# Adapter kernel on one core: who issues the loads of W_up, who writes the first seed, when the sort's tail runs, and the order of work in the first tiles

## The reference

```python
Wd = W_down[stream]; bd = b_down[stream]; Wu = W_up[stream]
bu = b_up[stream]; g = ln_w[stream]; b = ln_b[stream]
h = jnp.einsum('bsh,bhk->bsk', hidden_states, Wd) + bd[:, None, :]
h = jax.nn.gelu(h, approximate=False)
h = jnp.einsum('bsk,bkh->bsh', h, Wu) + bu[:, None, :]
h = residual + h                     # residual = hidden_states
mean = jnp.mean(h, axis=-1, keepdims=True)
var = jnp.mean(jnp.square(h - mean), axis=-1, keepdims=True)
h = (h - mean) * jax.lax.rsqrt(var + LN_EPS)
return h * g[:, None, :] + b[:, None, :]
```

## Time and profile before

| | before |
|---|---|
| median of 3 runs | 139.09 us (139.05 to 139.56) |
| profiled execution, its own time | 139.21 us |
| its span, first to last instruction | 137.2 us |
| mean granted PE clock | 0.987 of full speed |
| PE busy | 126.6 us (92%) |
| DVE busy | 112.9 us (82%) |
| POOL busy | 104.5 us (76%) |
| ACT busy | 85.1 us (62%) |

### The profile page before, as it was taken

One profiled execution on the slowest core, in us unless ns is written; L12 is line 12 of the kernel. 1 busy time (PEld: TensorE's weight loads), 2 busy tenths in 40 slices (PEclk: granted clock), 3 DMA queues, 4 the chain that ended last, 5 costly groups with the idle time before them and its releaser, 6 DMA issues.

```text
span 137.2 us, 4086 instructions
## 1 busy us (share of the span) xinstructions
PE 126.6 (92%) x850; PEld 112.5 (82%) x851; DVE 112.9 (82%) x273; ACT 85.1 (62%) x177; POOL 104.5 (76%) x117
## 2 busy tenths in 40 slices
PE   6788799999899999999999999999999999999830
PEld 6687667799799999999999999999999999998610
DVE  1899588788898888888988897889788978897992
ACT  0768576536966666666676666666666666666600
POOL 7047933438599888888888888888888898889960
PEclk9999999999999999999999999999999999999995
DMA  1967999995554354554555545455556533331365
GB/s 45 336 203 244 272 259 280 286 232 159 151 166 133 99 151 153 155 155 153 153 155 153 153 155 153 153 153 153 153 153 158 148 76 76 81 76 38 87 163 176
DMA packets 13200, 21.94 MB, mean 160 GB/s; under 512 B 2297, under 2 KB 3842, under 8 KB 13186
## 3 DMA queue, kind: packets, MB, share of 16 engines
q1 hardware_dynamic: 8802, 15.74, 41.6%
q10 hardware_dynamic: 4384, 6.05, 14.5%
HBM read 13.39 MB, written 8.65 MB: 161 GB/s over the span
## 4 chain that ended last, share of the span: by engine, by line
PE 70%; DVE 11%; POOL 6%; ACT 5%; issue 3%; DMA 2%; POOLq 1%; ACTq 1%; DVEq 0%
PE hg_ps L891 28%; PE y_ps L923 28%; PE xT_ps L877 8%; PE hg_ps L900 5%; POOL res L396 2%; DMA itok_all_i<-in_itok_B_dram 2%; DVE r_stats L704 1%; ACT xT_hi L463 1%; DVE hb L692 1%; ACT y_ps L480 1%; DVE res L740 1%; DVE scaled L725 1%; POOL slot_same L367 1%; POOL slot_step L366 1%; POOLq L210 1%
## 5 line engine op out<-in xcount | busy, mean ns | idle before, releaser
L396 POOL TENSOR_TENSOR res<-normed,lnb_rows 128x512 f32<-128x512 f32 x31 | 39.8, 1285 | 11.9 <-ACT normed L488 11.9
L379 POOL TENSOR_TENSOR xb<-x_sb,bu_rows 128x512 f32<-128x512 f32 x33 | 42.7, 1296 | 2.9 <-DMA x_sb<-in_x_dram 2.3
L468 ACT ACTIVATE g<-hb 128x256 f32<-128x256 f32 x33 | 13.8, 418 | 35.7 <-DVE hb L692 35.7
L704 DVE BATCH_NORM_STATS2 r_stats<-y_ps 128x6 f32<-128x512 f32 x33 | 23.0, 696 | 6.8 <-issue 6.1
L923 PE MATMUL y_ps<-wu_hi,gT_hi 128*128 x66 | 23.3, 434 | 1.4 <-ACT gT_hi L473 1.2
L684 DVE TENSOR_TENSOR xT_lo<-xT_ps,xT_hi 128x512 fp32r<-128x512 f32 x33 | 22.8, 690 | 2.1 <-ACT xT_hi L463 2.1
L385 POOL TENSOR_TENSOR rstd<-var_eps,half_neg 128x1 f32<-128x1 f32 x33 | 18.2, 551 | 7.9 <-DVE var_eps L713 7.8
L891 PE MATMUL hg_ps<-wd_hi,xT_hi 128*128 x132 | 24.1, 304 | 0.0
L725 DVE SCALAR_TENSOR_TENSOR scaled<-y_ps,r_mv,lnw_rows 128x512 f32<-128x512 f32 x31 | 22.9, 743 | 0.0
L488 ACT ACTIVATE normed<-scaled,rstd 128x512 f32<-128x512 f32 x31 | 22.3, 722 | 0.0
L891 PE MATMUL hg_ps<-wd_lo,xT_hi 128*128 x132 | 21.0, 282 | 0.0
(11 more groups left out here) (88 smaller groups left out, 148.0 us busy)
## 6 DMA issues: line engine op xcount, KB each, us to landing
x_sb<-in_x_dram SPq DMA_DIRECT2D x64, 128.0 KB, 2.8
out_dram<-res ACTq DMA_DIRECT2D x33, 128.0 KB, 2.4
out_dram<-res SPq DMA_DIRECT2D x33, 128.0 KB, 2.5
wd<-in_L_cond_W_down_dram ACTq DMA_DIRECT2D x3, 512.0 KB, 4.9
wu<-in_L_cond_W_up_dram SPq DMA_DIRECT2D x3, 512.0 KB, 6.3
lnw_rows<-in_L_cond_ln_w_dram SPq DMA_DIRECT2D x1, 768.0 KB, 7.9
lnb_rows<-in_L_cond_ln_b_dram SPq DMA_DIRECT2D x1, 768.0 KB, 9.3
x_sb<-in_x_dram ACTq DMA_DIRECT2D x2, 128.0 KB, 2.8
```

The lines of the kernel that those rows point to most:

```text
L379: pool.tensor_tensor(xb[:, c % DEEP, :], x_sb[:, c % FAR, :], bu_rows[:, ds(e * H, H)], ALU.add).then_inc(xb_ready, 1)
L396: pool.tensor_tensor(res[:, c % FAR, :], normed[:, c % DEEP, :], lnb_rows[:, ds(e * H, H)], ALU.add).then_inc(res_ready, 1)
L704: dve.bn_stats(r_stats[:, c % DEEP, :], y_ps[c % YBANKS][:]).then_inc(stats_ready, 1)
```

## The change

1. **Loads of W_up.** ACT issues all three, behind its two halves of x and behind wd_high(2) in program order. For their experts it reads seven table entries, `io_table[5:12]`, with one register load ahead of wd_high(2); DVE now writes the experts to free third entries of `io_table` instead of `wu_from`. SP reads twelve entries with one register load and issues x for tiles 2 to 5 in a row.
2. **First seed.** DVE writes seed(0), behind down_bias(0); it has a semaphore of its own, `seeded_first`. w_up_low(0) and g_lo(0) follow, then down_bias(1).
3. **Sort's tail.** POOL does add_bias for tiles 0, 1 and 2 first, then the six instructions of the tail.
4. **Order in the head.** ACT: wu_high(1) is ahead of gelu(1), x_hi(3) ahead of gelu(2); g_hi(5), gelu(6), x_hi(8) and seed(6) stand ahead of rescale(2) and rescale(3). DVE: stats(0) comes after g_lo(1) and x_lo(3); mean_var(1) and variance(1) come after x_lo(4). PE: up(1) and up(2) take the products in the usual order; two warm-up matmuls ahead of down(0) are gone.

The core of the diff:

```diff
@@ -295,22 +295,16 @@
 
 
             head_regs = [sp.alloc_register(f"head{i}") for i in range(4)]
-            from_regs = [sp.alloc_register(f"from{i}") for i in range(E)]
+            next_regs = [sp.alloc_register(f"next{i}") for i in range(12)]
 
             sp.wait_ge(slots_ready, 1)
             sp.reg_load(head_regs, io_table[0:1, 0:4])
             for t in range(2):
                 load_half(sp, t, 0, sp.snap(head_regs[3 * t], min_val=0, max_val=B - 1))
             sp.wait_ge(slots_ready, 2)
-            sp.reg_load(from_regs, wu_from[0:1, 0:E])
-            from_expert = [sp.snap(reg, min_val=0, max_val=E - 1 - slot) + slot for slot, reg in enumerate(from_regs)]
-            load_w_up(sp, 0, from_expert[0])
-            load(2, 2, entries(2, 0, 2))
-            load_w_up(sp, 1, from_expert[1])
-            load(3, 3, entries(3, 0, 2))
-            load_w_up(sp, 2, from_expert[2])
-            for t in range(4, 6):
-                load(t, t, entries(t, 0, 2))
+            sp.reg_load(next_regs, io_table[0:1, 5:17])
+            for t in range(2, 6):
+                load(t, t, [sp.snap(reg, min_val=0, max_val=B - 1) for reg in next_regs[3 * t - 5:3 * t - 3]])
             sp.dma_start(lnw_rows[:], rows_of(ln_w, P)).then_inc(lnw_in, 16)
             load(6, 6, entries(6, 0, 2))
             sp.dma_start(lnb_rows[:], rows_of(ln_b, P)).then_inc(lnb_in, 16)
...
+            pool.wait_ge(slots_ready, 2)
+            pool.wait_ge(bu_last_ready, 1)
+            pool.wait_ge(bu_ready, E - 1)
+            for t in range(3):
+                add_bias(t, t)
+
...
-            for t in range(3):
-                add_bias(t, t)
             add_bias(3, 3)
...
@@ -518,24 +515,28 @@
             wd_high(1)
             for t in range(2):
                 load_half(act, t, 1, act.snap(head_regs[3 * t], min_val=0, max_val=B - 1))
+            from_regs = [act.alloc_register(f"from{i}") for i in range(3 * E - 2)]
+            act.wait_ge(slots_ready, 2)
+            act.reg_load(from_regs, io_table[0:1, 5:3 * E + 3])
             wd_high(2)
+            for slot in range(E):
+                load_w_up(act, slot, act.snap(from_regs[3 * slot], min_val=0, max_val=E - 1 - slot) + slot)
             for e in range(E - 1):
                 keep_up_bias(e)
             x_hi(0, 0)
             x_hi(1, 1)
             for part in range(len(bd_banks)):
                 keep_down_bias(part)
-            seed(0, 0)
             wu_high(0)
             gelu(0, 0)
             g_hi(0, 0)
             x_hi(2, 2)
+            wu_high(1)
             gelu(1, 1)
-            wu_high(1)
             seed(1, 1)
             g_hi(1, 1)
+            x_hi(3, 3)
             gelu(2, 2)
-            x_hi(3, 3)
             wu_high(2)
             g_hi(2, 2)
             seed(2, 2)
@@ -556,24 +557,26 @@
             x_hi(7, 7)
             seed(5, 5)
             rescale(1, 1)
+
+            g_hi(5, 5)
+            gelu(6, 6)
+            x_hi(8, 8)
+            seed(6, 6)
             rescale(2, 2)
+            rescale(3, 3)
 
             def body(t, c):
 
                 seed(t, c)
-
-                if from_tile(t, 2):
-                    g_hi(t - 1, c - 1)
-                if from_tile(t, STORE_B_LAG):
-                    store(t - STORE_B_LAG, c - STORE_B_LAG)
+                g_hi(t - 1, c - 1)
+                store(t - STORE_B_LAG, c - STORE_B_LAG)
                 gelu(t, c)
                 x_hi(t + 2, c + 2)
-                if from_tile(t, 3):
-                    rescale(t - 3, c - 3)
+                rescale(t - 3, c - 3)
 
             act.wait_ge(slots_ready, 3)
-            for t in range(STORE_B_LAG, STORE_B_LAG + 2):
-                body(t, t)
+            store(0, 0)
+            body(STORE_B_LAG + 1, STORE_B_LAG + 1)
             tiles(act, body, STORE_B_LAG + 2, TILES - 3)
...
             dve.memset(io_table[0:1, 2:3], 0)
+            dve.memset(io_table[0:1, 14:15], 0)
...
@@ -649,7 +653,7 @@
             link(dve.tensor_scalar(tile_expert[:], key_filled[:, 1:1 + SLOTS:2], B.bit_length() - 1, RANGE // B - 1,
                                    ALU.logical_shift_right, ALU.bitwise_and))
 
-            dve.tensor_tensor(wu_from[:], first_expert, top_row[:], ALU.min)
+            dve.tensor_tensor(io_view[:, 1:1 + E, 2], first_expert, top_row[:], ALU.min)
...
@@ -745,28 +749,29 @@
             x_lo(1, 1)
             dve.wait_ge(bd_ready, len(bd_banks))
             down_bias(0, 0)
-            down_bias(1, 1)
+            dve.wait_ge(xb_ready, 1)
+            dve.tensor_copy(y_ps[0][:], xb[:, 0, :]).then_inc(seeded_first, 1)
             w_up_low(dve, 0).then_inc(wu_lo_ready, 1)
             g_lo(0, 0)
+            down_bias(1, 1)
             x_lo(2, 2)
-
-            stats(0, 0)
-            dve.wait_ge(stats_ready, 1)
             w_up_low(dve, 1).then_inc(wu_lo_ready, 1)
             down_bias(2, 2)
             g_lo(1, 1)
+            x_lo(3, 3)
+
+            stats(0, 0)
+            dve.wait_ge(stats_ready, 1)
+            w_up_low(dve, 2).then_inc(wu_lo_ready, 1)
             mean_var(0, 0)
+            g_lo(2, 2)
             variance(0, 0)
-            x_lo(3, 3)
-
+            down_bias(3, 3)
             stats(1, 1)
             dve.wait_ge(stats_ready, 2)
-            w_up_low(dve, 2).then_inc(wu_lo_ready, 1)
-            g_lo(2, 2)
+            x_lo(4, 4)
             mean_var(1, 1)
-            down_bias(3, 3)
             variance(1, 1)
-            x_lo(4, 4)
             scale(0, 0)
...
@@ -903,20 +910,16 @@
             def up(t, c, e):
 
                 w0 = e * (KB * H)
-                early = isinstance(t, int) and 0 < t < E
                 pe.wait_ge(ghi_ready, t + 1)
                 if isinstance(t, int) and t < E:
                     pe.wait_ge(wu_hi_ready, t + 1)
-                pe.wait_ge(seeded, t + 1)
-                parts = [(gT_hi, wu_hi), (gT_lo, wu_hi), (gT_hi, wu_lo)] if early else [
-                    (gT_hi, wu_hi), (gT_hi, wu_lo), (gT_lo, wu_hi)]
-                for n, (g_half, w_half) in enumerate(parts):
-                    if w_half is wu_lo and isinstance(t, int) and t == 0:
-                        pe.wait_ge(wu_lo_ready, 1)
-                    if w_half is wu_lo and isinstance(t, int) and t == 1:
-                        pe.wait_ge(wu_lo_ready, 2)
-                    if w_half is wu_lo and isinstance(t, int) and t == 2:
-                        pe.wait_ge(wu_lo_ready, 3)
+                if isinstance(t, int) and t == 0:
+                    pe.wait_ge(seeded_first, 1)
+                else:
+                    pe.wait_ge(seeded, t)
+                for n, (g_half, w_half) in enumerate(((gT_hi, wu_hi), (gT_hi, wu_lo), (gT_lo, wu_hi))):
+                    if w_half is wu_lo and isinstance(t, int) and t < E:
+                        pe.wait_ge(wu_lo_ready, t + 1)
                     if g_half is gT_lo:
                         pe.wait_ge(glo_ready, t + 1)
...
@@ -928,10 +931,10 @@
             pe.wait_ge(slots_ready, 2)
             transpose_x(0, 0)
             transpose_x(1, 1)
-            warm_up(WARM_UPS[3], hg_ps[0])
             pe.wait_ge(wd_hi_ready, E)
             down(0, 0, expert_of(pe, 0))
             e0, e1 = experts_from(0)
+            e_up, e_down = experts_from(1, next_regs)
             pe.wait_ge(bd_ready, len(bd_banks))
```

More of the change, by code:

```diff
@@ L56, in adapter_program @@
     EARLY = 3
-    WARM_UPS = 10, 4, 3, 2
+    WARM_UPS = 10, 4, 3
     with ExitStack() as ctx:
@@ L74, in adapter_program @@
         top_row = sb("top_row", [1, E], I32)
-        wu_from = sb("wu_from", [1, E], I32)
         ones = sb("ones", [P, P])
@@ L193, in adapter_program @@
         bu_ready = sem("bu_ready")
+        seeded_first = sem("seeded_first")
         seeded = sem("seeded")
@@ L362, in mark @@
                 pool.wait_ge(marking, steps)
-            pool.wait_ge(rows_ready, 2)
-            pool.tensor_copy(slot_batch_f[:], slot_batch[:]).then_inc(marking, 1)
-            mark(pool.tensor_tensor(slot_step[:], key_f[:, 1:1 + SLOTS], key_f[:, 0:SLOTS], ALU.subtract), 2)
-            mark(pool.tensor_scalar(slot_same[:], slot_step[:], 0.0, float(B), ALU.is_equal, ALU.mult), 3)
-            mark(pool.tensor_tensor(slot_step[:], slot_same[:], slot_batch_f[:], ALU.add), 4)
-            mark(pool.tensor_copy(slot_store[:], slot_step[:]), 5)
-            pool.tensor_copy(io_table[:].rearrange("p (t n) -> p t n", n=3)[:, STORE_A_LAG:, 2],
-                             slot_store[:, 0:SLOTS:2]).then_inc(slots_ready, 1)
             def add_bias(t, c):
@@ L376, in add_bias @@
                 pool.wait_ge(x_in[c % FAR], landed_count(t, c))
-                if from_tile(t, DEEP):
-                    pool.wait_ge(seeded, t - DEEP + 1)
+                if isinstance(t, int) and t == DEEP:
+                    pool.wait_ge(seeded_first, 1)
+                elif from_tile(t, DEEP):
+                    pool.wait_ge(seeded, t - DEEP)
```

(16 more changed lines are left out.)

## The result

| | before | after |
|---|---|---|
| median | 139.07 us (138.96 to 139.56, 4 runs) | 141.44 us (140.91 to 142.34, 4 runs) |
| ratio to before | | 1.0145 (0.95 interval 1.0094 to 1.0196) |
| profiled execution: time, span | 139.21, 137.2 us | 142.34, 140.6 us |
| its mean granted PE clock | 0.987 | 0.973 |

The kernel became 1.45% slower. The forecast, 139.7 us with a range to 141.0, had the side right and the size wrong. The four runs of after differ in the clock: spans of 139.1, 139.5, 139.8 and 140.6 us stand beside mean clocks of 0.989, 0.982, 0.982 and 0.973.

The account below looks back on a forecast made before the run. PE alone bounds the kernel from up(6) on, so only the head could change: +0.6 - 0.6 + 0.2 + 0.3 + 0.1 = +0.6 us, giving 139.7 us by the median, range 138.4 to 141.0.

Parts of the forecast that it names:

- What bounds the kernel: From up(6) on PE alone sets 3.48 us a tile; the change can only move when PE enters that state.
- ACT's front end: Head: ACT's register load of seven entries costs 1.2 us (0.36 to 2.0) and three DMA issues 1.9, ahead of x_hi(0).
- What the front of the head gives back (Term 1): Front of the head, to down(2): +0.6 us net; -0.2 with the load at 0.36, +1.4 with 2.0.
- The clock rival: Clock falls in PE's gap ahead of down(0), so down(0) and down(1) take twice: +2 to +3, 142; chance 0.10.
- W_up was not late: Rival: W_up's slot 1 comes late or w_up_low(1) waits for xb(3), adding 0.7 to 1: 140.5; chance 0.15.
- The rival in which the head's gain survives: Faster, 138.3 us, needing the register load at 0.36, w_up_low(0) at 1.23 and rescales no worse; chance 0.18.
- PE's register load for tile 1: On PE in the head, moved ahead of down(1): -0.1 us at most.
- Terms 2, 3 and 5: Middle of head: w_up_low(2) sooner after down(2), -0.6; down_bias(3) later, +0.2; rescales moved, g_hi(6) later, +0.1 us.
- The tight spot: Rescales on ACT: PE's tight spot moves from up(5) to up(6); g_hi(6) 0.5 later, mostly taken by slack of 0.4.
- Term 4: down_bias(3) to scale(0) on DVE: mean_var(1) and variance(1) now stand on the path, +0.3 us.
- SP's load "delays nobody": SP's single load of twelve entries, 1.1 to 3.4 us, holds up nothing: x of tile 2 is needed after 17 us.
- The lock on w_up_low(0): DVE's w_up_low(0) against POOL's xb: 1.7 us taken, from 1.93 beside two xb and 1.23 with POOL idle.

Follow-up runs that it names:

- the run with warm-ups: The changed kernel with eight warm-up matmuls added behind transpose_x(1): 141.77 us, ratio 1.0173.
- part 1 alone: The kernel before with only ACT asking for W_up behind its load of seven entries, and SP's one load of twelve: 141.13 us, ratio 1.0146.
- loads at four: The changed kernel with both long register loads starting at a multiple of four (ACT eight entries, SP sixteen): 140.35 us, ratio 1.0068.

## Why the prediction was wrong

**What bounds the kernel:** right. The rate from up(6) on is unchanged, and the head's 3.37 us arrive whole.

**ACT's front end:** the mechanism was right, and so was each order of events; the size of the load was short. The register load was taken as 1.2 us, with 2.0 as the upper bound, and took 1.56. The reading of the earlier trace rows, that the entries at a multiple of four in the middle go as a group, failed: the load from entry 5 cost 223 ns for each of seven. The three issues were taken as 1.9 and took 1.70. The bias copies came at 12.71 instead of 12.3, x_hi(0) at 13.67 instead of 13.3, down(0) at 14.41 instead of 13.9. By the Trainium skill's rule of some 200 ns a register (Runtime: NRT & Kernel Launch, Instruction fetch mechanics) the seven would be 1.4 us, nearer than the 1.2 that was taken; the run of loads from entry 4 contradicts it, with 70 ns an entry.

**What the front of the head gives back (Term 1):** this is the step that failed: forecast +0.6 us, measured +3.0 in the profiled execution. Some 0.5 of the difference is down(0) itself, at 14.41 instead of 13.9. The larger part lies behind it: down(2) was to follow down(0) by 6.1 us and followed by 7.96. Of the 1.9 us of error, 1.35 is the clock (the run with warm-ups, 6.61), and the other 0.5 is in what stood between at full clock. There the row shows PE waiting 0.93 us behind its register loads; that it makes up the 0.5 is an inference from the 0.5 us that its removal gave elsewhere.

**The clock rival**, given 0.10, is what happened in the profiled execution and, by the mean clock, in three of the four. The reasoning went by the earlier trace rows, where the clock was still full 1.6 us after the last matmul, and took a gap of 1.9 us as "just short" of the fall. One row of the tail was stretched to a rule. PE had nothing for 1.78 us ahead of down(0) and the clock fell, less than 1.4 us after the last matmul (12.64), where in the tail it was still full after 1.6; in part 1 alone PE had nothing for 1.53 us and the clock stayed up. And by the mean clocks one kernel goes either way from one execution to the next (after: 0.973 to 0.989; loads at four, with 1.13 us of nothing: 0.978 to 0.997). So the length of the gap alone does not tell. Its price was put at 2 to 3 us; it measured 1.35 in the profiled execution and about 0.4 in the median. That its 142 lies beside the 142.34 of that execution is luck. So the rival had the wrong chance and the wrong size, and even it doesn't explain the result: at full clock the span is 139.25, which with 1.8 us outside gives 141.0, the very end of the range.

**The other rivals.** W_up was not late: wu_high(0) started at 15.37 with no wait ahead of it, and where w_up_low(1) met xb(3) it was POOL that waited (2.31 us instead of 1.29). The rival in which the head's gain survives was given 138.3 if the register load took 0.36 us. With the load at 0.56 us the kernel measured 140.35, and down(2) was still 0.6 us later than before, at 19.95 against 19.36: the issues stay ahead of x_hi(0), and the earlier w_up_low(0) met POOL's third xb.

**"PE's register load for tile 1: -0.1 at most"** had the wrong sign: +0.5, by the two versions in which SP asks for W_up.

**Terms 2, 3 and 5** held in sign, and 3 and 5 in size: -0.91, +0.27 and +0.14 for -0.6, +0.2 and +0.1. The tight spot moved to up(6), with PE waiting 0.78 us, as the prediction said.

**Term 4** was mis-sized: +0.86, for +0.3. It counted two small instructions and not the register load of scale(0) queued behind them.

**SP's load "delays nobody"** was not quite so: it took 2487 ns, x of tile 2 was only asked for at 12.77 us behind other work of SP's, and POOL's xb(2) waited 0.86 us for x. No run shows that this reached the end.

**The lock on w_up_low(0)** was priced at 1.7 us and took 1.97 (2.26 where POOL's third xb has just started, 1.22 where SP asks for W_up and it starts ahead of that xb). The Trainium skill's rule on DVE and POOL in SBUF (SBUF — State Buffer, Who interferes with whom), by which the second of the two stands still until the first is done, agrees with these three: the long ones started while an xb was running, and beside the one of 1.22, which started first, POOL's xb took 1.99 us.

## What to carry to other kernels

An instruction that moves to another engine brings its front-end work with it: count the register load and every DMA issue at the engine that gets them, and ask which instruction behind them is awaited. Here 3.3 us of such work stood ahead of x_hi(0), on the one engine that PE waited for. A register load belongs in a place where the engine has long work in its queue, not ahead of or right behind a short instruction that someone waits for; here this was worth 0.5 us on PE at full clock, and 0.5 to 1.0 us, together with mean_var and variance, on DVE. And filling a wait with small work is free only while the wait is there.
